# A binarised sublayer split between two attention plans, and ternary weight pieces placed only between exponentials

## The reference

```python
x = _layernorm(x + _L2_attn_ref(x, L2_attn_w_qkv, L2_attn_w_out))      # sublayer 4
x = _layernorm(x + _L2_ffn_ref(x, L2_ffn_weight, L2_ffn_bias))         # sublayer 5
x = _layernorm(x + _L3_attn_ref(x, Wq, Wk, Wv, Wo))                    # sublayer 6
x = _layernorm(x + _L3_ffn_ref(x, W_up, W_gate, W_down))               # sublayer 7
```

## Time and profile before

| | |
|---|---|
| median of three timed runs | 1154.64 us (1154.28 to 1155.13) |
| the profiled execution | 1155.26 us, span 1153.4 us |
| TensorE busy | 1001.0 us, 87% |
| VectorE / ScalarE / GpSimd busy | 716.9 / 527.2 / 331.9 us |
| mean granted TensorE clock | 0.895 |
| attention 4 | about 629 to 837 us of the span |
| sublayer 5 | about 837 to 867 us |
| attention 6 | about 863 to 1087 us |

### The profile page before, as it was taken

One profiled execution on the slowest core, in us unless ns is written; L12 is line 12 of the kernel. 1 busy time (PEld: TensorE's weight loads), 2 busy tenths in 40 slices (PEclk: granted clock), 3 DMA queues, 4 the chain that ended last, 5 costly groups with the idle time before them and its releaser, 6 DMA issues. The chain is left out here.

```text
span 1153.4 us, 16469 instructions
## 1 busy us (share of the span) xinstructions
PE 1001.0 (87%) x5914; PEld 569.1 (49%) x5914; DVE 716.9 (62%) x2013; ACT 527.2 (46%) x1131; POOL 331.9 (29%) x464
## 2 busy tenths in 40 slices
PE   6999998888889877899999999997757988888795
PEld 2544554774344445437437544444443544445584
DVE  1667773877597894531432467777291588777585
ACT  3566656431566872210110557664304355565432
POOL 3211112331376871000000221112461054432142
PEclk8989999988586876899999889999877899999897
DMA  6000000103000000200000020000000000000001
GB/s 232 1 1 1 1 1 1 51 1 162 18 1 2 1 1 2 106 0 1 1 0 1 1 109 2 2 1 1 1 0 1 1 1 1 1 2 1 1 1 37
DMA packets 4324, 21.60 MB, mean 19 GB/s; under 512 B 377, under 2 KB 1657, under 8 KB 3220
## 3 DMA queue, kind: packets, MB, share of 16 engines
q1 hardware_dynamic: 4244, 20.55, 4.7%
HBM read 19.01 MB, written 1.05 MB: 17 GB/s over the span
## 5 line engine op out<-in xcount | busy, mean ns | idle before, releaser
L901 ACT ACTIVATE PB<-pair 128x1024 f32<-128x1024 f32 (+3 forms) x288 | 223.2, 811 | 135.3 <-PE pair L1638 133.8
L1139 DVE CUSTOM_DVE_ANT_0 junk<-bank,cst 128x128 bf16<-128x128 f32 (+3 forms) x384 | 171.2, 487 | 114.6 <-PE bank L1622 112.3
L734 POOL TENSOR_SCALAR_AFFINE_SELECT PB<-PB 128x256 f32<-128x256 f32 x192 | 79.0, 414 | 327.4 <-ACT PB L901 325.1
L1142 DVE TENSOR_REDUCE pmx<-bank 128x1 f32<-128x512 f32 x192 | 122.7, 684 | 55.9 <-PE bank L1622 54.8
L1622 PE MATMUL bank<-KO_r,QO_r 64*128 64x512 f32 (+3 forms) x576 | 140.2, 417 | 11.1 <-DVE A L1217 3.9
L1654 PE MATMUL pvb<-PB,V 128*32 128x512 f32 (+3 forms) x1152 | 125.3, 507 | 10.8 <-ACT PB L901 8.0
L1622 PEld LDWEIGHTS bank<-KO_r,QO_r 64*128 64x128 f32 x576 | 71.5, 189 | 113.6 <-DVE pmx L1139 38.9
L1634 PE MATMUL pair<-QO_r,KO_r 64*128 64x512 f32 (+3 forms) x576 | 114.3, 387 | 12.7 <-ACT PB L901 11.5
L740 POOL TENSOR_TENSOR parts_r<-y_f,parts_r 128x512 fp32r<-128x512 f32 x24 | 30.7, 1280 | 314.4 <-ACT parts_r L872 314.4
L955 ACT ACTIVATE KO<-pair,nm 128x128 f32<-128x128 f32 x256 | 90.0, 385 | 42.0 <-DVE nm L1302 41.9
L1638 PE MATMUL pair<-ms,sel_r 64*128 64x512 f32 (+3 forms) x576 | 101.0, 343 | 0.0
(11 more groups left out here) (211 smaller groups left out, 1708.0 us busy)
## 6 DMA issues: line engine op xcount, KB each, us to landing
WF<-in_moe_gu SPq DMA_DIRECT2D x1, 3520.0 KB, 11.2
WA<-in_w_att SPq DMA_DIRECT2D x3, 1024.0 KB, 9.4
WF<-in_tern_w SPq DMA_DIRECT2D x1, 3072.0 KB, 10.1
V<-in_moe_d SPq DMA_DIRECT2D x1, 1792.0 KB, 7.3
xT<-in_xT SPq DMA_DIRECT2D x2, 512.0 KB, 5.8
X<-in_x SPq DMA_DIRECT2D x1, 1024.0 KB, 10.5
A<-in_rope SPq DMA_DIRECT2D x1, 1024.0 KB, 4.7
out<-X SPq DMA_DIRECT2D x2, 512.0 KB, 2.9
```

Source lines behind the costliest of these rows:

```text
L734: pool.affine_select(p2, p2, pattern=[[0, 2], [1, P]], compare_op=ALU.is_ge, fill=0.0, base=0, channel_multiplier=-1).then_inc(causal, 1)
L901: act.activation(pb[:, st % 2, 2 * i:2 * i + 2, 0:n], ps[:, :, 0:n], ACT.Exp, scale=scale)\
L1139: r_done(dve.tensor_tensor_reduce(junk[:, (r_used - 1) % 3, 0:n], ps[:, 0:n], tri[:, HALF - n:HALF], 1.0, LOWEST, ALU.add, ALU.max, accum_ ...
L1142: r_done(dve.tensor_reduce(to, ps[:, 0:n], AX.X, ALU.max))
```

## The change

- **Early half of sublayer 5** (half 1): new items in attention 4's list behind `new`: `bin` 0 to 3 (a tile each, with residual and bias), `bin_norm`, `bin_new` (transposes and copies).
- **Late half** (half 0): new items in attention 6's list: `late_x` at place 4 (transposes of sublayer 4's late half), `late` 0 to 3 and `late_norm` behind two further selector items. Nothing of sublayer 5 stands between the lists any more.
- **Operands of attention 6** in another order: all of the early half first (four `b`, eight `s` with `late` among them, `v` 2 and 3), then `x1`, then the late half's. VectorE's clock in the planner starts at 16000 ns.
- **Normalised tiles** are counted in the new order (`xn_at`): sublayer 4's late half counts behind sublayer 5's early half.
- **Weights:** items 0 and 1 move to the front of `accT` of (3,1); 2 to 5 stay.
- **Ternary pieces:** none before attention 6; one behind each `exp` that is not on the diagonal in a stage with half 1, which are 32 places; the other four behind the list.

The core of the diff:

```diff
+def xn_at(s, k):
+    if SUBLAYERS[s:s + 2] == (ATT, BIN):
+        return NT * s + TH * (2 * k + 1)
+    if SUBLAYERS[s] == BIN:
+        return NT * s + TH * 2 * k
+    return NT * s + TH * (k + 1)
...
+    if BIN in SUBLAYERS[s - 1:s]:
+        ready = [x for x in early + late if x[0] in "bs" and x[3] == first] + [("v", k) for k in range(first * 2, first * 2 + 2)]
+        return ready + [("x1",)] + [x for x in early + late if x not in ready and x != ("x1",)]
...
+    if BIN in SUBLAYERS[s - 1:s]:
+        clock.dve = 16000
...
+                if SUBLAYERS[s + 1] == BIN:
+                    out.extend([("bin", k) for k in range(TH)] + [("bin_new",)])
...
+    if BIN in SUBLAYERS[s - 1:s]:
+        plan[4:4] = [("late_x",)]
+        plan[7:7] = [("late", k) for k in range(TH)] + [("late_norm",)]
     if s == 4:
-        at = plan.index(("accT",) + STAGES[-3])
-        plan[at:at] = [("weights", n) for n in range(6)]
+        for stage, items in ((STAGES[-3], range(2, 6)), (MIXED, range(2))):
+            at = plan.index(("accT",) + stage)
+            plan[at:at] = [("weights", n) for n in items]
...
-                        elif item[2] and item[3] < TH - 1:
+                        elif item[2]:
                             next(between, None)
...
             pieces = ternary()
-            for _ in range(5 * 3):
-                next(pieces)
             attention(6, pieces)
...
+                    if item[0] == "bin":
+                        residual(s + 1, TH * halves_in(s + 1)[0] + item[1])
+                    if item[0] == "bin_norm":
+                        normalise(s + 1, 0)
+                    if item[0] == "late":
+                        residual(s - 1, TH * halves_out(s - 1)[1] + item[1])
+                    if item[0] == "late_norm":
+                        normalise(s - 1, 1)
...
-                pe.wait_ge(xn_ready, NT * s + TH * (halves_out(s).index(half) + 1))
+                pe.wait_ge(xn_ready, xn_at(s, halves_out(s).index(half)))
...
+                    if item[0] == "bin":
+                        if item[1] == 0:
+                            pe.wait_ge(bin_ready, 1)
+                            x_ready(halves_in(s + 1)[0])
+                        project_tile(TH * halves_in(s + 1)[0] + item[1], WB)
+                    if item[0] == "bin_new":
+                        new_x(s + 1, halves_out(s + 1)[0])
+                    if item[0] == "late_x":
+                        new_x(s - 2, halves_out(s - 2)[1])
+                    if item[0] == "late":
+                        half = halves_out(s - 1)[1]
+                        x_ready(half)
+                        project_tile(TH * half + item[1], WB)
...
-                else:
-                    pe.wait_ge(bin_ready, 1)
-                    first, second = halves_in(s)
-                    x_ready(first)
-                    project_out(s, first, WB)
-                    new_x(s - 1, second)
-                    x_ready(second)
-                    project_out(s, second, WB)
-                    new_x(s, first)
```

More of the change, by code:

```diff
@@ L173, in span, with operands @@
     return q0, (qh + 1) * HALF - q0
-def operands(first, second):
+def operands(s, first, second):
     def build(kind, side, g, half):
@@ L291, in issue @@
                 done["norm"] = clock.dve + clock.FREED
+        elif kind == "bin":
+            clock.tensor(start, 900)
+            clock.vector(1300)
+            if item[1] == TH - 1:
+                plan.append(("bin_norm",))
+                clock.dve += 4200
+                done["bin_norm"] = clock.dve + clock.FREED
         elif kind == "b":
```

31 lines of the change are left out of this document (16 added, 15 removed).

## The result

| | before | after |
|---|---|---|
| median, 8 runs each, taken together | 1154.83 us (1153.52 to 1155.84) | 1149.79 us (1149.13 to 1153.21) |
| ratio to before, 95% interval | | 0.9965 (0.9955 to 0.9975), 4.0 us |
| profiled execution, span | 1153.4 us | 1151.3 us |
| mean granted clock of TensorE | 0.895 | 0.891 |

The profile of the changed kernel was taken on the slowest of its eight executions, 1153.21 us; the other seven took 1149.13 to 1150.91 (mean clock 0.893 to 0.896), so its rows show more of the low clock than a usual execution has.

The account below looks back on a forecast made before the run. TensorE (busy 87%) bound the kernel, but VectorE did from 834.6 to 862.7 us and a relay to 887. -0.3 - 4.2 - 10.0 + 1.8 = -12.7 us took 1154.64 to 1141.9, say 1142.0; range 1136 to 1150.

Parts of the forecast that it names:

- rival 1: TensorE's clock stays low before attention 6's first scores: gain only about 5 us, 1149.5 us; chance 0.13.
- signs of a wrong forecast: First maximum after 887, clock below 0.8 from 850 to 880, or kb = 4 causal selections starting later than their exponentials.
- Step A: Weight items 0 and 1 moved earlier: the wait moves, its end doesn't; -0.3 us, bounds -1 and +1.5.
- Step B: Early half inside attention 4: 4.6 us added on TensorE, transposes of A at 836.2; bounds 3.5 and 5.5.
- Step C: From the transposes of A to attention 6's first score maximum: 883.0 against 887.19, -4.2 us, bounds -7 and 0.
- rival 3: GpSimd's port contention with VectorE in attention 6 costs 6.5 us instead of 1.8: 1146.7 us; chance 0.08.
- Step D: First scores to stage (0,1)'s first exponential: 12.9 us of products leave TensorE; -10 us, bounds -13 and -6.
- Step E: Ternary instructions moved into and behind attention 6 cost VectorE's port there: +1.8 us, bounds 0 and +4.
- the milder reading of the contention: Added GpSimd instructions slow only some VectorE instructions; the skill's rule in full meant about 3 us less gain.

Follow-up runs that it names:

- weights_back: The changed kernel with weight items 0 and 1 put back beside items 2 to 5, as before; 0.9972 of the kernel before, 1149.1 us.
- warm: The changed kernel with 62 small products into a bank nobody reads, at fourteen places in or near TensorE's waits; 0.9882, 1140.8 us.
- before_tern: The kernel before with the ternary part of the change alone; 0.9979, 1150.5 us. With fillers in TensorE's waits (before_tern_warm): 0.9898.
- early_only: The changed kernel with the late half back between the two attention lists and attention 6's operands in the old order; 0.9985, 1152.0 us.
- fit: The changed kernel with only two V products (4 us) of the early half's 13.5 us ahead of the late transposes; 0.9895, 1141.7 us.
- before_warm: The kernel before with fillers in front of TensorE's waits between 828 and 886 us; 0.9944, 1147.7 us.
- early_warm: The kernel early_only with fillers in TensorE's waits between 832 and 883 us; 0.9895.
- v_later: The changed kernel with the products of V 0 and V 1 one place later, behind the first and second pair of first scores; 0.9957.
- tail_pieces: The changed kernel with the first four ternary instructions right behind attention 4 instead of the last four behind attention 6; 0.9955.
- fit_none: The changed kernel with none of the early half's 13.5 us of products between the late tiles and late transposes; 0.9967, 1150.5 us.
- fit_tail: The kernel fit with the edit of tail_pieces; 0.9898, 1141.9 us.

## Why the forecast was right in direction and wrong in size

**What was right.** Faster was right. The kind of rival 1, a clock that stays low, came true; it had 0.13. Its number, 1149.5 us beside a measured 1149.8, was met in part by luck. It put 6.4 us on the three pairs of base products, and these ran at the full level (3.60, 3.60 and 3.70 us). Others were slow in their place: the projection, the late tiles, the V products. Two of my signs of a wrong forecast came: the first maximum behind 887 (889.3 on the scale), and a clock below 0.8 from 850 to 880 (0.77).

**Step A** (-0.3): the reductions start at 803.7 on the scale, before at 804.37; weights_back agrees in time. Right.

**Step B** (+4.6, bounds 3.5 and 5.5): the transposes of A come at 835.6 on the scale, 4.0 later than before. Right; accumulator (2,0) was in time, as argued.

**Step C** (-4.2, bounds -7 and 0): +2.2. This is the step that failed, by 6.4 us. The term that was mis-sized is the price of TensorE's products between the transposes of A and the first maximum: I took the full level of the clock for them, since "it comes out of a stretch at 0.94". The positions of the step show where the time went:

| on the scale, us | forecast | changed kernel | with fillers (warm) |
|---|---|---|---|
| transposes of A | 836.2 | 835.6 | 836.1 |
| transposes of sublayer 4's late half | 850 | 851.5 | 849.4 |
| first late tile | 853.2 | 855.4 | 852.0 |
| late normalisation ready | 864.0 | 869.5 | 864.6 |
| transposes of the late half | 870.5 | 875.4 | 868.2 |
| first maximum | 883.0 | 889.3 | 879.7 |

In the changed kernel the projection ran 2.5 us over its price and the late tiles 2.3 over theirs, and VectorE's late normalisation, which waits for both, came 5.5 late. With the clock held every position is within 3.3 us of the forecast, four of the six within 1.2, and step C is -7.5. So the order of work in my sum was right and its clock was wrong. The sum also mixed two clocks: it held the changed kernel at the full level against a kernel before that ran its base pairs at 5.74 and 6.17 us. That difference was measured too, warm against the kernel before without fillers: 0.9882, 13.6 us, near the 12.7 that I forecast. Held for both, it is about 7.

What each part of the change did to the first maximum, by single profiles, whose clock differs by 2 to 3 us:

- The relief from GpSimd's 15 instructions: -7.1 (before_tern), -5.6 at a held clock. I had 5.5 us for it in rival 3's account, more than the whole -4.2.
- The early half on top: +1.5 (early_only against before_tern).
- The late half on top: +5.6 in weights_back, +7.7 in the changed kernel, +7.0 at a held clock. This cost stood in my sum: "So VectorE's chain is hidden by 6 us; what is late now is TensorE's own operand relay". Products that end 6 us after the work they hide are no cover, they are the path. VectorE's row at 869.93 and TensorE's at 877.16 show these 6 us. They don't explain why the number was missed, but they are why the late half gains so little.

**Step D** (-10, bounds -13 and -6): from the first maximum to the end of stage (0,1) 43.9 us instead of 51.7, -7.8. In bounds; the 12.9 us of products taken out gave 0.6 us for each us. fit gives the same from the other side: 6.9 us of products put back cost 5.8. What I did not see is that C and D are one account: the products taken out of D were the ones put into C.

**Step E** (+1.8, bounds 0 and +4): from (0,1) to the end of the span the lead shrinks from 5.7 to 3.9 us, +1.8 (before_tern: 3.1). Right. What the same edit gave stood in step C, so that I never set its gain against its cost and missed that it was a large part of the change.

The sum by the rows: +2.2 - 7.8 + 1.8 = -3.8 (A and B are in C), against 3.9 in the spans on the scale. That the ratio says 4.0 as well is in part luck: the rows are of the changed kernel's slowest execution, and the two profiled times themselves are 2.1 us apart.

**The port.** I took the milder reading of the contention between GpSimd and VectorE for the instructions that are added, and it held (rival 3 did not come). It was the removed ones that I under-read. In the kernel before a normalisation L1090 took 2.76 and 2.35 us beside the pieces and 1.38 alone, and in the changed kernel GpSimd's low parts hold VectorE in the same way: two steps on 4 elements took 1.20 us while L772 ran, against 0.16.

```profile
848.83 1.28 POOL L772 TENSOR_TENSOR parts_r<-y_f,parts_r 128x512 fp32r<-128x512 f32 x1 [14.25 <-ACT parts_r L902]
...
848.93 1.20 DVE L1105 SCALAR_TENSOR_TENSOR lnv<-lnv 128x4 f32<-128x4 f32 x1
...
850.17 0.16 DVE L1103 SCALAR_TENSOR_TENSOR lnv<-lnv 128x4 f32<-128x4 f32 x1
```

The Trainium skill ("SBUF — State Buffer", section "Who interferes with whom") has two-input instructions of VectorE contend with GpSimd instructions that read SBUF; these steps, L1105 beside the subtraction L772, agree. L1090, which has one tensor input and two columns of scalars, was held as well, by the two times above.

## What to carry to other kernels

Before you fill a wait with moved work, find how long the wait is once everything else in the same change is in place: work moved into it is free up to that length, and beyond it is only moved from one side of the next milestone to the other. Try each part of a change alone, the one that looks like a side condition first: here silencing GpSimd beside a chain on VectorE was at a held clock the larger part of the gain, and the two sides of the late half came near to cancelling. When you price work on TensorE, price both kernels at the same level of the clock. And where TensorE waits for a relay in pieces of 1 us, a few products that nobody reads can be worth more than a better order.

## What the runs showed of the hardware

**Filler products pay.** Fillers are the small products of warm. A row of before_warm, in the wait that was 6.22 us before:

```profile
840.03 4.97 PE L1555 MATMUL pair<-wmaskb,idb 128*128 128x256 bf16 x44
```

That is 0.113 us each, and 62 of them took 9.6 us off the changed kernel, by the ratios. In warm, before_warm, early_warm and before_tern_warm the granted clock is 1.00 in 834 to 864 and in 864 to 890, where the kernels without them have 0.61 to 0.93. More of them at three other waits, with the edits of v_later and tail_pieces, brought about 5 us more (0.9882 to 0.9840).

**The same instructions at either level.** Up to the projection behind attention 4 the changed kernel, v_later, fit_none, fit and tail_pieces, fit_tail have the same TensorE program, with the same waits of 0.71, 0.88 and 0.69 to 0.74 us in front. In the first three and in tail_pieces the sixteen products took 6.18 to 6.26 us, in fit and fit_tail 3.72. The Trainium skill ("TensorE: Matmul & The Clock Gate", Part 1) says that "the default state is throttled, and activity releases the throttle" and that the number of slow products at the start of one kernel differs from run to run. Here such a difference shows within one kernel and not only at its start: the 87 executions of the kernel before that were timed beside the experiments took 1150.4 us at a mean clock of 0.901 to 1158.2 at 0.892, the slower the lower the clock (on the average 1153.0 at 0.898, 1156.3 at 0.894). So differences of 2 to 3 us between two orders of work, read from one profile each, may be the clock's. Only one execution of each kernel has rows, so whether the level of a given stretch goes with the build or with the execution stays open. For fit it does not look like the execution alone: ten of the twelve executions of fit and fit_tail have a mean clock of 0.903 or more, all eight of the changed kernel 0.896 or less. Why fit fell on the good side, and the kernels with 13.5 us and with none on the bad one, no run here settles.
